# Attention on one core: units of 1024 columns in one ring of three double PSUM banks, and key and query parts spread by DMA

## What is computed

```
b, t, c = x.shape            # 2, 2048, 256
nh, hd = (NH, c // NH)       # 16, 16
...
scores = jnp.einsum('bhtd,bhsd->bhts', q, k) / math.sqrt(hd)
attn = jax.nn.softmax(scores, axis=-1)
out = jnp.einsum('bhts,bhsd->bhtd', attn, v)
```

## Time and profile before

| | |
|---|---|
| runs of the kernel (3) | median 4231.87 us, from 4230.5 to 4232.61 |
| profiled execution, first to last instruction (its span) | 4296.5 us |
| PE / PEld busy in the span | 82% / 43% |
| DVE / ACT / POOL busy in the span | 58% / 49% / 27% |
| attention core, first transpose to last sum | 130 us to 1759 us of the span |

### The profile page before, as it was taken

One profiled execution on the slowest core, in us unless ns is written; L12 is line 12 of the kernel. 1 busy time (PEld: TensorE's weight loads), 2 busy tenths in 40 slices (PEclk: granted clock), 3 DMA queues, 4 the chain that ended last, 5 costly groups with the idle time before them and its releaser, 6 DMA issues. The chain is left out here.

```text
span 4296.5 us, 115371 instructions
## 1 busy us (share of the span) xinstructions
PE 3510.7 (82%) x41173; PEld 1852.0 (43%) x41175; DVE 2485.8 (58%) x5229; ACT 2102.7 (49%) x4024; POOL 1149.9 (27%) x2368
## 2 busy tenths in 40 slices
PE   8699999999999999732396977550869699898999
PEld 5232222322323222332264644440757566544678
DVE  7788888888888888580021238457245433235433
ACT  2488888888888888421143434320610022264322
POOL 1222222222222221124505844510533123210000
PEclk9799999999999999866698988555965599898999
DMA  1000000000000002534346533344723300233353
GB/s 53 7 6 6 6 6 7 6 6 6 6 7 6 6 6 89 189 102 139 136 137 195 161 118 124 122 140 150 246 84 75 86 15 0 84 135 125 108 188 125
DMA packets 288679, 345.07 MB, mean 80 GB/s; under 512 B 36768, under 2 KB 201632, under 8 KB 288544
## 3 DMA queue, kind: packets, MB, share of 16 engines
q1 hardware_dynamic: 254736, 297.27, 21.7%
q0 software_dynamic: 13328, 37.77, 2.7%
q10 hardware_dynamic: 20480, 8.40, 0.7%
HBM read 198.11 MB, written 135.79 MB: 78 GB/s over the span
## 5 line engine op out<-in xcount | busy, mean ns | idle before, releaser
L945 DVE TENSOR_REDUCE att_maxes<-att_ps_m 128x1 f32<-128x512 f32 x2048 | 1308.5, 686 | 230.9 <-PE att_ps_m L789 225.2
L900 ACT ACTIVATE att_prob<-att_ps_s 128x512 f32<-128x512 f32 x2048 | 1105.6, 599 | 222.5 <-PE att_ps_s L799 209.9
L799 PE MATMUL att_ps_s<-att_q_t,att_k_t 99*128 99x512 bf16 x2048 | 687.2, 386 | 8.7 <-ACT att_prob L900 7.9
L810 PE MATMUL att_ps_o<-att_prob,att_v_h 128*32 128x512 f32 x4096 | 546.4, 605 | 0.7 <-ACT att_prob L900 0.7
L787 PE MATMUL att_ps_m<-att_k_t,att_q_t 48*128 48x512 bf16 x1024 | 398.8, 389 | 16.3 <-DVE att_maxes L945 11.5
L789 PE MATMUL att_ps_m<-z_sb 48*128 48x512 bf16 x1024 | 399.3, 390 | 0.0
L787 PEld LDWEIGHTS att_ps_m<-att_k_t,att_q_t 48*128 48x128 bf16 x1024 | 94.6, 92 | 610.3 <-DVE att_maxes L945 509.8
L1570 DVE TENSOR_TENSOR experts_h<-experts_gs,experts_ps_g 128x128 f32<-128x128 f32 x192 | 55.3, 288 | 497.4 <-ACT experts_gs L1551 423.5
L698 POOL CAST att_max_parts<-att_neg_max 128x4 bf16<-128x4 f32 x128 | 24.9, 194 | 1154.1 <-DVE att_neg_max L952 1154.1
L799 PEld LDWEIGHTS att_ps_s<-att_q_t,att_k_t 99*128 99x128 bf16 x2048 | 157.7, 96 | 281.0 <-ACT att_prob L900 134.4
L1523 PE MATMUL experts_ps_g<-w_gu,experts_x_t 128*128 x768 | 225.1, 417 | 54.8 <-issue 41.0
(11 more groups left out here) (357 smaller groups left out, 6472.0 us busy)
## 6 DMA issues: line engine op xcount, KB each, us to landing
xf_t<-logits_t SPq DMA_DIRECT2D x16, 2048.0 KB, 8.5
slots_x<-zeros SPq DMA_DIRECT2D x97, 256.0 KB, 3.3
experts_xs<-slots_x SPq DMA_DIRECT2D x48, 512.0 KB
slots_y<-experts_y SPq DMA_DIRECT2D x48, 512.0 KB
logits_t<-sstat_logit SPq DMA_DIRECT2D x64, 256.0 KB
proj<-comb_pr SPq DMA_DIRECT2D x8, 1600.0 KB
mix_pr<-proj SPq DMA_DIRECT2D x32, 400.0 KB
gram_qk_in<-proj SPq DMA_DIRECT2D x32, 256.0 KB
```

The lines of the kernel that those rows point to most:

```text
L799: pe.matmul(ps_s[bank(p, i)][:, :], k_t[0:ROWS, p, tile * P:(tile + 1) * P], q_t[0:ROWS, p, chunk * W:(chunk + 1) * W], start=True, stop=T ...
L810: mm = pe.matmul(ps_o[i * VW:(i + 1) * VW, :], v_h[:, p, group * GK + i, :], prob[:, (j * GK + i) % (RING * GK), :], start=(group == 0), s ...
L900: nc.scalar.activation(prob[:, i % (RING * GK), :], ps_s[bank(p, i)][:, :], ACT.Exp, scale=SCALE).then_inc(expd.sem, 1)
L945: v.tensor_reduce(maxes[:, p, tile, c:c + 1], ps_m[bank(p, i)][:, :], X, ALU.max).then_inc(reduced.sem, 1)
```

## The change

The units of both passes become 1024 columns wide: two matmuls into a double bank, and one reduction or one exponential over both. The six banks become one ring of three double banks that both passes use in turn (`score_bank`, `pass_bank`): score unit i takes the double bank of first-pass unit i − 2, and first-pass unit i that of score unit i − 1. PE's order in a step becomes: score unit, turn, first-pass unit, score unit, `against_v` of the step before, first-pass unit.

POOL no longer writes repeated parts. Three parts of the queries and three of the keys lie side by side in one stack of 96 columns, are turned together (two turns in a head in place of four), and are copied by ACT to `parts_t`. SP then spreads the rows to their places in `q_t`, `k_t`, `q_low` and `k_low` with ten transfers for each half, twenty for a head, where three were. The rows of ones are set once in `k_t`. The turning of the output is no longer a transpose: it is a float32 matmul with `fold`, 128 rows by 32 columns, that also adds the four groups; DVE only copies the result.

```diff
-        ps_m = [ph.ps(f"ps_m{i}", [P, W]) for i in range(BANKS)]
-        ps_s = [ph.ps(f"ps_s{i}", [P, W]) for i in range(BANKS)]
+        ps_u = [ph.ps(f"ps_u{i}", [P, PAIR * W]) for i in range(BANKS)]
...
+        def score_bank(p, i):
+            return (2 * i + p) % BANKS
+
+        def pass_bank(p, i):
+            return (2 * i + 1 + p) % BANKS
...
+            def move(n, p, g):
+                sp.wait_ge(kept.sem, kept.at(n, g + 1))
+                part = slice(g * TG * P, (g + 1) * TG * P)
+                odd = slice(g * TG * P + W, (g + 1) * TG * P)
+
+                def copy(dst, src, rows, cols):
+                    sp.dma_start(dst[:, p, cols], parts_t[src:src + rows, p, cols]).then_inc(moved[g].sems[p], 32)
+
+                copy(q_t[0:2 * HD], Q + HD, 2 * HD, part)
+                copy(q_t[2 * HD:3 * HD], Q + 2 * HD, HD, part)
+                copy(q_low[0:2 * HD], Q + HD, 2 * HD, part)
+                copy(q_low[2 * HD:3 * HD], Q + 2 * HD, HD, part)
+                copy(k_t[0:HD], K, HD, part)
+                copy(k_t[HD:3 * HD], K, 2 * HD, part)
+                copy(k_low[0:HD], K, HD, odd)
+                copy(k_low[HD:3 * HD], K, 2 * HD, odd)
+                copy(q_t[3 * HD:6 * HD], Q, 3 * HD, part)
+                copy(k_t[3 * HD:6 * HD], K, 3 * HD, part)
...
+                if g == 3 and c < 2 and left >= 1:
+                    move(n + 1, 1 - p, c)
...
-                    mm = pe.transpose(ps_tro[:, i * P:(i + 1) * P], o_t[:, i * P:(i + 1) * P], ident[:, :])
+                    mm = pe.matmul(ps_tro[:, i * VW:(i + 1) * VW], o_t[:, i * P:(i + 1) * P], fold[:, :], start=True, stop=True)
...
+            def first_pass(n, p, m, bank):
+                tile, c = divmod(m, TU)
+                if m == 0:
+                    for both in moved:
+                        pe.wait_ge(both.sems[p], both.at(n, p))
+                c = c * PAIR
+                pe.matmul(ps_u[bank][:, 0:W], q_t[0:LEADING, p, tile * P:(tile + 1) * P],
+                          k_t[0:LEADING, p, c * W:(c + 1) * W], start=True, stop=True)
+                pe.matmul(ps_u[bank][:, W:PAIR * W], q_low[:, p, tile * P:(tile + 1) * P],
                           k_low[:, p, (c + 1) * W:(c + 2) * W], start=True, stop=True).then_inc(max_scores.sem, 1)
...
+            def seek(n, p, i, first):
+                if i == 0 and p == 0:
+                    pe.wait_ge(reduced.sem, reduced.at(n, AHEAD - 2 if first else AHEAD))
+                else:
+                    pe.wait_ge(expd.sem, expd.at(n, i))
+                first_pass(*sought(n, p, i), pass_bank(p, i))
...
+                m = i - 2 + AHEAD
+                if p == 0 and not first and i == 0:
+                    pe.wait_ge(expd.sem, expd.at(n, 0))
+                elif p == 0 and not first and i == 1:
+                    pe.wait_ge(reduced.sem, reduced.at(n, m))
+                elif m < UNITS:
+                    pe.wait_ge(reduced.sem, reduced.at(n, m + 1))
...
+                for r in range(PAIR):
+                    tile = group * GK + q * PAIR + r
+                    mm = pe.matmul(ps_u[score_bank(p, i)][:, r * W:(r + 1) * W], k_t[0:ROWS, p, tile * P:(tile + 1) * P],
+                                   q_t[0:ROWS, p, chunk * W:(chunk + 1) * W], start=True, stop=True)
+                mm.then_inc(scores.sem, 1)
...
                 if left >= 0:
-                    score(n, p, j, 0)
+                    score(n, p, j, 0, left, first)
                 turns()
+                if seeks:
+                    seek(n, p, j * US, first)
                 if left >= 0:
-                    score(n, p, j, 1)
-                seek(0)
-                if left >= 0:
-                    score(n, p, j, 2)
+                    score(n, p, j, 1, left, first)
                 if j:
                     if left >= 0:
                         against_v(n, p, j - 1)
                 elif not first:
                     against_v(n - 1, 1 - p, STEPS - 1)
-                seek(2)
-                if left >= 0:
-                    score(n, p, j, 3)
+                if seeks:
+                    seek(n, p, j * US + 1, first)
...
-                v.tensor_reduce(maxes[:, p, tile, c:c + 1], ps_m[bank(p, i)][:, :], X, ALU.max).then_inc(reduced.sem, 1)
+                v.tensor_reduce(maxes[:, p, tile, c:c + 1], ps_u[bank][:, :], X, ALU.max).then_inc(reduced.sem, 1)
```

More of the change, by code:

```diff
@@ L550, in phase_attention @@
         divided = ph.sem("divided")
-        k_moved = ph.transfers("k_moved")
-        q_moved = [ph.transfers(f"q_moved{g}_") for g in range(2)]
+        moved = [ph.transfers(f"moved{g}_", MOVES) for g in range(2)]
         block = ph.block()
@@ L796, in score @@
                     pe.wait_ge(max_kept.sem, max_kept.at(n, chunk + 1))
-                pe.wait_ge(expd.sem, expd.at(n, freed(p, i)))
-                tile = group * GK + q
-                pe.matmul(ps_s[bank(p, i)][:, :], k_t[0:ROWS, p, tile * P:(tile + 1) * P],
-                          q_t[0:ROWS, p, chunk * W:(chunk + 1) * W], start=True, stop=True).then_inc(scores.sem, 1)
+                m = i - 2 + AHEAD
[5 more added lines that the diff above has]
+                    pe.wait_ge(reduced.sem, reduced.at(n, m + 1))
+                elif left >= 1:
+                    pe.wait_ge(reduced.sem, reduced.at(n + 1, m + 1 - UNITS))
+                else:
+                    pe.wait_ge(expd.sem, expd.at(n, i - 2))
@@ L893, in keep_output, with exponentials @@
                 nc.scalar.copy(o_t[:, :], ps_o[:, :]).then_inc(o_kept.sem, 1)
-            def exponentials(n, p, j, first, last):
-                for i in range(j * GK + first, j * GK + last):
-                    act.wait_ge(scores.sem, scores.at(n, i + 1))
-                    if i == j * GK:
-                        act.wait_ge(pv.sem, pv.at(n, j - RING + 1))
-                    nc.scalar.activation(prob[:, i % (RING * GK), :], ps_s[bank(p, i)][:, :],
-                                         ACT.Exp, scale=SCALE).then_inc(expd.sem, 1)
+            def exponentials(n, p, j, q):
+                i = j * US + q
+                slot = i * PAIR % (RING * GK)
+                act.wait_ge(scores.sem, scores.at(n, i + 1))
+                if q == 0:
+                    act.wait_ge(pv.sem, pv.at(n, j - RING + 1))
+                nc.scalar.activation(prob[:, slot:slot + PAIR, :].rearrange("q a w -> q (a w)"), ps_u[score_bank(p, i)][:, :],
+                                     ACT.Exp, scale=SCALE).then_inc(expd.sem, 1)
             def step(n, h, p, j, left, first):
```

220 lines of the change are left out of this document (79 added, 141 removed).

## The result

The changed kernel takes a median of 4364.63 us (4363.3 to 4366.75, 4 runs) beside 4231.18 us for the kernel before in the same comparison: 1.0321 times as long, with a 95% interval of 1.0306 to 1.0335, or +133.4 us. The prediction said 4350 us, slower. Both the direction and the mechanism came out; the forecast was 15 us short. Two terms of it were too small (the output turn and the start), and one step under it, on recording, was wrong without harm.

The account below looks back on a forecast made before the run. PE was taken as a full queue, DVE and ACT as having slack. Steady chunks 113, ring changes 5, start 2, end −2 gave +118 us on 4232: 4350 us, own range 4318 to 4382; 4290 to 4400 at 0.8.

Parts of the forecast that it names:

- The ring: Shared double banks: release takes 1.71 us against 1.18 of PE work; stall 0.53, period 3.25 us a step.
- P2: Second first-pass unit of a step, last in PE's order; put at 0.32 us of PE's work.
- S2: Second score unit of a step; to wait 0.53 us, without a turn, for the reduction of the previous step's P2.
- routing row: Profile row of routing's 16 float32 instructions, 0.114 us each; eight such put the output turn at 0.91 us.
- S1: First score unit of a step, first in PE's order; put at 0.54 us of PE's work.
- Edits that I cost at nothing: Exponentials, ACT's copies, `find_max` and its turn, POOL's dropped copies, twenty transfers: all put at zero cost, covered by spare time.
- break of the ring: At 15 changes from p = 1 to p = 0 another unit waits; S2 comes 0.33 us later, +5 us.
- The start: Before attention's first score: twenty issues (10.4 us), partly offset by dropped work; 0 to +8 us, taken as +2.
- The fold is cheap: Rival: output turn stays 0.47 us, every step 3.25, chunk 13.00, total 4302 us; chance 0.10.
- The reduction is in time: Rival at S2's wait: 1024-column reduction takes 0.70 us or less, PE stays full, 4206 us, faster; chance 0.08.
- Transfers late: Rival: at 1.2 us an issue, transfers come 2 us late in 31 heads, +65 us, 4415; chance 0.05.
- The clock falls: Rival: PE's gaps lower TensorE's clock to 1.2 GHz; one chunk in ten gives +100 us, 4450; chance 0.05.

Follow-up runs that it names:

- stack alone: Kernel before with one stack, two turns a head and twenty transfers; units, banks, order and output turn as before: 4221.63 us, 0.9981.
- halved reduction: Changed kernel with each reduction reading only 512 of its 1024 columns, everything else kept: 4224.65 us, 0.9989 of the kernel before.

## Why the prediction was right, point by point

**The loss is shared out.** In medians: stack alone −8.6 us; wide units and ring on top of it +88.6 (4310.2 − 4221.6); the fold on top of these +54.4. That they add up to the whole is no proof, since each is taken on top of the one before. The proof for the fold is that it was also measured by itself, at +52.3: it costs 0.40 us a chunk in the ring (13.46 − 13.06) and 0.42 outside it. The stack is another matter. Its two turns fewer were worth 0.13 us a chunk in the old order, and in the ring turns of this kind hide in the stall, so the +88.6 holds the loss of that saving too.

**What bounded the kernel: right.** The yardstick of 2.72 us for PE's own work in a step holds: with the halved reduction an ordinary step runs from `against_v` at 803.07 to that at 805.79, 2.72 us. The forecast that DVE and ACT have slack and that relieving them gains nothing is borne out: for each chunk DVE is busy 10.0 us instead of 10.7 and ACT 9.8 instead of 10.6, and the kernel got slower.

**The ring: right to the hundredth.** 1.71 us from P2 to S2 and a period of 3.25, both as worked out. Only the sign to look for was drawn too simply: a gap of half a microsecond stands in one step of three (107 of 311) and not in three of four, because the turns fill part of it, as the prediction's own section on them says. The price of the reduction, drawn from the slope between 272 and 512 columns, was 1.23 us; it is 1.224. The halved reduction shows the cause: with the same columns through PE, the same ring and the same list, the stall is gone and so are 140 us (about 5 of them at the start, where the reductions are shorter too).

**The turns: right in kind, the output turn undersized in the ring.** The routing row gave 0.91 us; the trace shows 0.89 when a score follows. In the changed kernel a pair follows, and the turn takes 0.98; at 833.01 it takes 1.01, but starts 0.45 behind S1 and not 0.54. So the step is 3.70 or 3.64 us where 3.63 was put, and over 126 chunks that is about 8 us, half of what the sum at the end of attention lacked.

The runs show two things behind the size. With ACT's copy as late as it is here, the turn takes 0.89 us when a score follows and 0.98 when a pair does. With the copy moved ahead (the experiment with `against_v` ahead of S2), S1 and the turn together take 1.35 us instead of 1.52 although a pair follows; the sum had 0.54 + 0.91 = 1.45. So the term that failed stands under "Edits that I cost at nothing": ACT's copies fit into ACT's own time, but the turn waits for the end of this one. The kernel before has the same wait (0.11 us from the copy's end to the load), so the 0.54 us that the prediction read from 813.11 to 813.65 is not all PE's own price. A fixed price for a change of kind doesn't explain these numbers alone; what a pair behind the turn costs by itself no run measured.

The statement on which the cheap fold leaned, that transpose mode is four times faster for FP32 (the Trainium skill, "TensorE: Matmul & The Clock Gate", section "Terms"), is weighed by the two runs with both forms. With the transposes four weight loads take 0.42 us, with the fold eight take 0.97. A plain float32 matmul is two instructions, and each one loads 128 weight columns at about 0.11 to 0.12 us, however few columns it then moves. By the statement as the prediction used it, a quarter of the columns would have made up for it. Here it did not, because the loads fill the whole turn.

**A chunk** was put at 13.38, with the break of the ring 13.42, and is 13.46 by the count in the windows view, 13.48 by the starts of `against_v`. Over 126 chunks these starts give +126.1 us where 118 was put. The break was put at 0.33 and is 0.31.

**The start: a term that was mis-sized.** I took +2 of a range of 0 to +8; it is +8.1, at the end of the range. It is made up of four parts. Attention's first memset starts 1.5 us later, which is not the change's doing. From there to POOL's first split it is 5.59 us instead of 1.08 (+4.5): the rows of ones are now 3 partitions of 2048 columns, each such memset takes 1.76 us, and POOL waits for the last of the set-up. From the split to the first first-pass pair it is 21.89 instead of 14.07 (+7.8): the twenty issues stand 0.63 us apart where the earlier trace rows showed 0.52 for one, so they take 12.7 us and not 10.4, and the last one's data is used 2.3 us after its issue, which the term left out. From the pair to the first score it is 13.52 instead of 19.26 (−5.7): shorter reductions and a turn that fell away, where the prediction named 1 us for the reductions.

**These add up.** From the first score to the end of attention the changed kernel is 126.0 us longer (134.1 − 8.1), where 113 + 5 − 2 = 116 was put. About 8 of the 10 are the steady chunks. The rest is the end: the last steps were put at −2, and between the 505th start of `against_v` and the last one only 0.4 us are won.

**The step from span to runs: wrong, and harmless.** The prediction took the 65 us between span and runs for a cost of recording, and the text on the kernel before says so. The span of the changed kernel is no longer than its runs. Set side by side, the 65 us sit in the experts' phase: from its first transposes to its last it took 520.6 us in that one execution of the kernel before, 457.1 in the changed kernel, and 449.9 to 458.9 in the eight experiments. Attention had none of it, so the sum could be set against the runs anyway; that this cost nothing was luck. What made that execution slow there is open.

**The rivals.** *The fold is cheap* fell: 54.4 and 52.3 us. *The reduction is in time* fell with 1.224 us for it, and its point of decision (0.70) was confirmed by the halved reduction at 0.686. *Transfers late* fell: one wait for a transfer in all of attention, at its start, and seventeen more of them in a head of the old order at no cost in the steady stretch. The issue pitch of 0.63 us stays under the 1 us at which the spare was used up. *The clock falls* fell: 1.00, so 2.4 GHz, in the whole stretch, with PE idle for about half a microsecond in one step of three. What the Trainium skill reports of one kernel, that small gaps between groups of matmuls cycling through PSUM banks made the clock go up and down ("TensorE: Matmul & The Clock Gate", section "A second HAM failure mode: psum-queue depth-cycling"), did not happen in this stretch, in which PE was busy for 981.52 of 1050 us.

## What to carry to other kernels

When two stages of a pipeline come to share one ring of banks, write down for each wait what the waiting engine has to do between the matmul that fills a bank and the one that needs it again, and set that against start delay, consumer and release: here 1.18 us against 1.71. Where the slower one is an engine with slack, its *latency* for one unit and not its load sets the time, so a wider unit can lengthen the loop while it lowers the busy share; a row with every engine less busy and a longer span is how that looks. When a stage behind PE hands data back to it, as ACT's copy does to the output turn, ask when the copy ends and not only whether its engine has room: moving it ahead shortened that step from 3.70 to 3.53 us. Try the parts of a bundle by themselves: one of the three was worth having, and a reordering next to it was worth more.

## What the runs showed of the hardware

- A float32 matmul that moves 32 columns through 128 weight columns costs no less than one that moves 64: 0.111 us for each of its two instructions (8 in 0.89 us) beside 0.114.
- A memset of 3 partitions by 2048 bf16 columns takes 1.76 us on DVE.
- Small transfers from SBUF to SBUF are issued every 0.63 us from SP's queue when they stand in a row; the last of twenty is issued at 152.08, and PE starts on its data at 154.35.
- A score costs 0.32 us when a first-pass pair follows, 0.21 when another score follows, and 0.22 to 0.24 when a turn on 128 rows follows that waits for nothing (two scores to the turn 0.44 with the copy moved ahead, 0.45 for half a stack).
- Moving the turns behind score 1 gained 31 us (0.9931) without one instruction less.
- Gaps of about 0.5 us in 107 of 311 steps left the granted clock at 1.00 for the whole stretch of 1050 us.
